# Local attention: the probabilities divided ahead of their transpose, the values held by the array, maximum and exponentials by halves

## The chip, the cores and the metric

One NeuronCore of one Trainium2 chip runs the whole program in one launch. The metric is the device time of that launch in microseconds. PE is TensorE, ACT is ScalarE, DVE is VectorE, POOL is GpSimd, SP is SyncE; PEld is the loading of the array's stationary operand. PSUM is used as four slots R[0] to R[3] of two banks each (128 partitions x 512 float32 a bank).

## The reference, cut to what matters

The program computes four parts one after the other for 32 batches of 128 tokens and 128 channels: a cross-attention, a routed layer of experts, a second cross-attention, and then two layers of the following, which are where the change is. HEADS = 8, DIM_HEAD = 64, WINDOW = 64, all in float32:

```python
h = shift_token(x)                       # second half of the channels from the token before
q, k, v = split(h @ wqkv, 3)             # 128 -> 3 x 512, 8 heads of 64
q, k = l2norm(q) * qs, l2norm(k) * ksc
q, k = rotary_xpos(q, k)
sim = einsum(q * 8, k)                   # per head, keys of this window of 64 and of the one before
sim = where(mask, -max, sim)
attn = softmax(sim)
o = einsum(attn, v)
x = x + o @ wo
# then layernorm of the shifted x, w1, a * gelu(g), w2, and the sum with x
```

The kernel takes each batch of 128 tokens as one 128 x 128 score matrix per head with an additive band mask.

## The kernel before

Each engine runs its own instruction stream, written out by hand, and waits on semaphores. A stage is a software pipeline over the 32 batches: step `i` runs `body(it)`, in which `it.b(lag)` is the batch `i - lag` (or None outside 0 to 31). So one step holds work of several batches, and the order of the blocks in `body` is the order on that engine. Nothing reorders it. The attention of one layer is the four functions `da_tensor`, `da_scalar`, `da_vector` and `da_pool` (and `da_sync` for the DMAs that shift the tokens). `l` is the layer. The layer's second half is `df_*`; `d_into_f` and `f_into_d` join them.

What happens to one batch, with the lag of each step:

- lag 0 to 1: z (the normed x) is written by DVE in the first layer (`d_zn`, L1787) and shifted by two DMAs; PE transposes it (L1650), ACT and DVE split it in a high part (L1719) and a low one (L1779); PE forms q and k in three passes for each half of 512 columns (L461 to L463, called for the columns 0 to 1023) in R[0]; ACT squares them (`d_sq`, L1748).
- lag 2: PE forms v in R[1] (`d_vp`), ACT copies it to SBUF (L1729). DVE multiplies q and k by the rotary tables: A (L1774, 1024 columns) and B in two halves (L1793, 512 columns each), after which it raises `d_rot` to its first count; it sums the squares (`d_ss`, L1810) and bounds them from below (`d_vv`, L1815, a tensor_scalar over 16 columns of SBUF). POOL adds B to A (L1855, waits for the first count of `d_rot`), takes the power -1/2 (L1859, waits for `d_vv`) and scales the keys (L1862).
- lag 4: PE transposes q and k into R[2] (L1630), ACT copies them (L1715), PE adds the band (L1666) and forms the scores of 8 heads in R[2] (L1669, 64 rows each). DVE takes the negated maximum (L1802) and scales it (`d_nm`, L1806). ACT makes the eight exponentials (L743, one per head).
- lag 5: PE transposes the exponentials P into R[3] (L1639), ACT copies them (L1723, `d_pT`). PE forms the product with v, with the transposed P as the stationary operand and v with a 65th column of ones as the moving one, 65 columns (L1686, `d_PV`). DVE takes the reciprocal of the 65th column (L1821) and multiplies the other 64 by it (L1823, `d_on`).
- lag 6: PE transposes the four 128-column pieces of `d_on` (L1680), ACT copies them (L1734, `d_oT`), PE multiplies by wo (L1704), DVE adds the result to Z (L1830).
- lag 7: DVE takes the statistics of the shifted row (L1762, L1038, L1040 `mv`), POOL their root (L1045).

A float32 matmul shows as two instructions of MATMUL, so 8 heads show as x16. A wait such as `e.wait_ge(S("d_exp"), count(b, base=B))` stops the whole engine until the batch `b` has been counted.

Of the kernel before, what the change touches and what calls it, by code (L numbers as in the profile page):

```python
# [112 lines left out]
def program(nc, out, x_in, ctx_in, mask_in, wq0_in, wkv0_in, wo0_in, nrm0_in, wg_in, w1e_in, w3e_in, w2e_in,  # L113
            l1_in, wqkv_in, qks_in, wol_in, lng_in, w1l_in, b1l_in, w2l_in,
            ident_in, band_in, rot_in, keyi_in, head_in):
    with ExitStack() as ctx:
# [184 lines left out]
        d["on"] = at("d_on", [128, 2, 512])  # L301
# [10 lines left out]
        d["v1"] = at("d_v1", [128, 4, HL, 65])  # L312
# [1237 lines left out]
        def c_pool(e):  # L1550
# [3 lines left out]
            e.memset(d["v1"][:, :, :, DL:DL + 1], 1.0).then_inc(S("d_con"), 1)  # L1554
# [62 lines left out]
        def da_tensor(e, l):  # L1617
            t, B = d, NB * l

            def body(it):  # L1620
                if it.static and it.i == 0 and l == 0:
                    e.wait_ge(S("split"), 8)
                    e.wait_ge(S("d_con"), 7)
                b = it.b(4)
                if b is not None:
                    if it.seen(5):
                        e.wait_ge(S("d_exp"), it.upto(5, B))
                    e.wait_ge(S("d_key"), count(b, 3, 3, base=B))
                    for c in range(8):
                        mm = e.transpose(R[2][:, c // 4, 128 * (c % 4):128 * (c % 4) + 128],  # L1630
                                         t["A"][:, it.m(4, 2), 128 * c:128 * c + 128], ident[:])
                    mm.then_inc(S("d_qkTp"), 1)
                b = it.b(5)
                if b is not None:
                    if it.seen(6):
                        e.wait_ge(S("d_div"), nth(it.upto(6, B), 2, 2))
                    e.wait_ge(S("d_exp"), count(b, base=B))
                    for c in range(8):
                        mm = e.transpose(R[3][:, c // 4, 128 * (c % 4):128 * (c % 4) + 128], t["p"][:, it.m(5, 2), c, :], ident[:])  # L1639
                    mm.then_inc(S("d_PT"), 1)  # L1640
# [11 lines left out]
                if b is not None:  # L1652
# [4 lines left out]
                    if it.seen(5):  # L1657
                        e.wait_ge(S("d_max"), nth(it.upto(5, B), 2, 2))
# [3 lines left out]
                if b is not None:  # L1662
# [8 lines left out]
                    mm.then_inc(S("d_S"), 1)  # L1671
                b = it.b(6)
                if b is not None:
# [543 lines left out]
```

## Time and profile before

| | |
|---|---|
| time, median of 3 runs | 1640.44 us (1639.03 to 1648.55) |
| the profiled execution | 1641.26 us; span of its instructions 1639.0 us |
| busy share of the span | PE 90%, PEld 74%, DVE 75%, ACT 68%, POOL 55% |
| granted TensorE clock, mean | 0.968 of full speed |
| chain that ended last | PE 55%, DVE 21%, ACT 7%, the rest under 6% each |

The two attention stages lie between about 900 and 1190 us and between about 1266 and 1565 us of the span. Busy shares are means over stages with different limits, so the rows further down are taken from inside these stages.

### The profile page before, as it was taken

How to read it: one execution, taken by the hardware profiler on the slowest of the kernel's cores; microseconds unless marked ns; L12 is line 12 of the kernel's file. 1: busy time of each engine (PE TensorE's matmuls, PEld its weight loads, DVE VectorE, ACT ScalarE, POOL GpSimd, SP SyncE). 2: the span in 40 equal slices, each digit the busy share in tenths (PEclk: the TensorE clock that was granted, in tenths of full speed). 3: DMA queues.
4: the chain of work that ended last, by engine and by line, in shares of the span. 5: the costliest groups of instructions: out<-in, count | busy, mean ns of one | idle time of the engine just before them, and what ended most of it. 6: DMA issues, size and time to landing. Idle time of an engine off the chain costs nothing.

```text
span 1639.0 us, 37579 instructions
## 1 busy us (share of the span) xinstructions
PE 1477.2 (90%) x11802; PEld 1206.1 (74%) x11803; DVE 1227.3 (75%) x3032; ACT 1112.5 (68%) x2666; POOL 908.3 (55%) x789
## 2 busy tenths in 40 slices
PE   4899999999878998898887899999989799999988
PEld 3677777777757876676665788888877688888866
DVE  6888888888755556878875688888765777878765
ACT  5878888877745556666665687787733687787732
POOL 5667778777740123444431777777600877777600
PEclk9999999999998997979998899999999999999999
DMA  9800000000022320110000000000000000000000
GB/s 382 314 2 7 11 10 11 11 12 16 14 62 68 88 72 21 59 37 21 21 18 10 11 15 15 15 14 15 11 12 4 6 16 14 16 14 15 11 19 38
DMA packets 87336, 62.62 MB, mean 38 GB/s; under 512 B 52037, under 2 KB 72901, under 8 KB 86469
## 3 DMA queue, kind: packets, MB, share of 16 engines
q1 hardware_dynamic: 83141, 53.00, 10.3%
q0 software_dynamic: 4096, 8.40, 1.7%
q8 instruction: 50, 0.82, 0.2%
q14 instruction: 49, 0.40, 0.1%
HBM read 21.30 MB, written 30.41 MB: 32 GB/s over the span
## 4 chain that ended last, share of the span: by engine, by line
PE 55%; DVE 21%; ACT 7%; issue 5%; SPq 5%; POOL 3%; DMA 3%; another core or an unknown queue 1%; DVEq 0%; POOLq 0%; ACTq 0%
PE slot L1686 6%; PE slot L461 5%; SPq L1328 5%; PE slot L463 4%; PE slot L462 4%; PE slot L1669 4%; PE slot L1630 4%; PE slot L1704 3%; PE slot L1639 3%; ACT a_p L743 3%; DMA c_vz<-c_v 3%; DVE a_sum L861 3%; PE slot L1939 2%; POOL a_rq L1106 2%; PE slot L1423 2%
## 5 line engine op out<-in xcount | busy, mean ns | idle before, releaser
L1045 POOL TENSOR_TENSOR rs<-mv,nhalf 128x1 f32 (+1 forms) x160 | 95.9, 599 | 262.0 <-DVE mv L1040 191.5
L1855 POOL TENSOR_TENSOR d_A<-d_A,d_B 128x1024 f32<-128x1024 f32 x64 | 150.9, 2358 | 132.5 <-DVE d_B L1793 132.4
L1859 POOL TENSOR_TENSOR d_r<-d_vv,nhalf 128x16 f32<-128x16 f32 x64 | 186.6, 2916 | 46.9 <-DVE d_vv L1815 46.4
L743 ACT ACTIVATE d_p<-slot,d_nm,d_r 128x128 f32<-128x128 f32 x512 | 186.0, 469 | 27.0 <-DVE d_nm L1806 27.0
L743 ACT ACTIVATE a_p<-slot,a_nm,a_rq 128x77 f32<-128x77 f32 x512 | 163.9, 433 | 57.1 <-DVE a_nm L768 57.1
L743 ACT ACTIVATE c_p<-slot,c_nm 128x77 f32<-128x77 f32 x512 | 117.4, 362 | 20.1 <-DVE c_nm L1478 20.1
L1686 PE MATMUL slot<-d_v,d_pT 128*128 128x65 f32 x1024 | 121.9, 272 | 1.7 <-ACT d_pT L1723 1.7
L1686 PEld LDWEIGHTS slot<-d_v,d_pT 128*128 128x128 f32 x1024 | 119.4, 192 | 2.4 <-ACT d_pT L1723 2.1
L750 POOL TENSOR_TENSOR a_p<-a_p,a_rc 128x616 f32<-128x616 f32 x64 | 80.1, 1252 | 71.2 <-DVE a_rc L863 70.7
L1774 DVE TENSOR_TENSOR d_A<-slot,T 128x1024 f32<-128x1024 f32 x64 | 78.3, 1224 | 47.5 <-PE slot L1630 47.5
L1802 DVE TENSOR_REDUCE slot<-slot 128x8 f32<-128x1024 f32 x64 | 78.9, 1233 | 27.8 <-PE slot L1669 25.1
L1448 ACT ACTIVATE c_pT<-slot 128x768 f32<-128x768 f32 x64 | 52.7, 823 | 67.2 <-PE slot L1370 67.2
L1106 POOL TENSOR_TENSOR a_rq<-a_vvq,nhalf 128x16 f32<-128x16 f32 x32 | 95.0, 2970 | 1.8 <-DVE a_vvq L978 1.8
L626 PE MATMUL slot<-a_kb,a_qT 128*128 128x154 f32 x512 | 81.4, 302 | 11.2 <-DVE a_pT L904 10.8
L1734 ACT ACTIVATE d_oT<-slot 128x512 f32<-128x512 f32 x64 | 38.2, 597 | 78.3 <-PE slot L1680 78.3
L1967 ACT ACTIVATE f_gl<-slot,b1l 128x512 f32<-128x512 f32 (+1 forms) x48 | 32.9, 685 | 77.6 <-PE slot L463 77.6
L1061 POOL DMA_INDIRECT routed<-r_xn,r_ps x64 | 65.0, 1015 | 35.5 <-issue 21.7
L1576 POOL DMA_INDIRECT c_yg<-answers,c_gi x64 | 63.9, 998 | 36.7 <-POOL c_gi L1572 25.5
L626 PEld LDWEIGHTS slot<-a_kb,a_qT 128*128 128x128 f32 x512 | 70.2, 191 | 18.9 <-DVE a_pT L904 17.8
L529 PE MATMUL slot<-ident,a_p 128*77 128x128 f32 x512 | 68.3, 277 | 15.6 <-POOL a_p L750 15.5
L1630 PE MATMUL slot<-ident,d_A 128*128 128x128 f32 x512 | 71.6, 284 | 11.6 <-ACT d_p L743 11.6
L1669 PEld LDWEIGHTS slot<-d_qT 64*128 64x128 f32 x1024 | 62.1, 187 | 27.0 <-issue 27.0
(288 smaller groups left out, 4563.7 us busy)
## 6 DMA issues: line engine op xcount, KB each, us to landing
routed<-zero SPq DMA_DIRECT2D x2, 9216.0 KB, 49.4
b_x<-routed SPq DMA_DIRECT2D x80, 64.0 KB
answers<-b_y SPq DMA_DIRECT2D x40, 128.0 KB
X<-in_x SPq DMA_DIRECT2D x2, 1024.0 KB, 7.2
d_zx<-Z SPq DMA_DIRECT2D x64, 32.0 KB
H<-Z SPq DMA_DIRECT2D x64, 32.0 KB
out<-f_o SPq DMA_DIRECT2D x8, 256.0 KB, 2.0
d_zx<-Z SPq DMA_DIRECT2D x64, 31.8 KB
```

The lines of the kernel that those rows point to most:

```text
L461: e.matmul(o, ws[1], xs[0], start=True, stop=False)
L626: mm = e.matmul(R[slot][:, k // 2, 2 * SK * (k % 2):2 * SK * (k % 2) + 2 * SK], a["qT"][:, c, :], a["kb"][:, it.m(2, 2), c // 2, :], start ...
L743: i = e.activation(t["p"][:, h, :], R[slot][:, k // nbank, nk * (k % nbank):nk * (k % nbank) + nk], ACT.Exp, bias=t["nm"][:, h:h + 1], sca ...
L750: return e.tensor_tensor(p, p, t["rc"][:, h].unsqueeze(2).to_broadcast([128, h.stop - h.start, nk]), ALU.mult)
L1045: return e.tensor_tensor(rs[:, bass.ds(b, 1)], mv[:, bass.ds(b, 1), 1:2].rearrange("p a b -> p (a b)"), nhalf[:, 0:1], ALU.pow)
L1106: e.tensor_tensor(a["rq"][:, it.m(1, 2), :], a["vvq"][:], nhalf[:, 0:16], ALU.pow).then_inc(S("a_rq"), 1)
L1328: e.dma_start(t["vz"][row:row + n, m, c, 32 * j:32 * j + 32], t["v"][key:key + n, m, 32 * j:32 * j + 32])\
L1630: mm = e.transpose(R[2][:, c // 4, 128 * (c % 4):128 * (c % 4) + 128], t["A"][:, it.m(4, 2), 128 * c:128 * c + 128], ident[:])
L1669: mm = e.matmul(R[2][:, h % 2, 128 * (h // 2):128 * (h // 2) + 128], t["qT"][o:o + DL, h // 2, :], t["qT"][o:o + DL, 4 + h // 2, :], start ...
L1686: mm = e.matmul(R[3][:, h // 4, 65 * (h % 4):65 * (h % 4) + 65], t["pT"][:, 4 * (h % 2) + h // 2, :], t["v1"][:, it.m(5, 4), h, :], start= ...
L1855: e.tensor_tensor(t["A"][:, p, :], t["A"][:, p, :], t["B"][:, p, :], ALU.add).then_inc(S("d_key"), 1)
L1859: e.tensor_tensor(t["r"][:, it.m(2, 4), :], t["vv"][:, p, :], nhalf[:, 0:16], ALU.pow).then_inc(S("d_key"), 1)
```

## The change

In each step of the local attention:

- The exponentials write out their sums (`accum_out`, tile `d_sum`), DVE inverts these (SBUF to SBUF), and multiplies the exponentials P themselves, 128 x 1024, in place. This is the first thing on DVE in a step and waits for all exponentials of the step before. `on`, the column of ones and its memset are gone.
- PE transposes P after the scores and not before them, waits for that product, and forms the product with v with v as the stationary operand (128 x 64) and the transposed P as the moving one (128 columns). The two heads of a pair go to partitions 0 to 63 and 64 to 127 of R[3], so the result is already the transpose that wo needs. The four transposes L1680 are gone. ACT copies it (as many columns as L1734). The product with v is now PE's last block of a step, behind the q and k projections.
- Maximum and `d_nm` are made for each bank of R[2], as are the exponentials; ACT copies the transposed P between the two halves, and PE starts each half of the next q and k transposes as soon as the exponentials of that half are done.
- On DVE the second half of B now follows the maxima, the low part of the transposed z follows the first half of B. POOL's code changes only in which count of `d_exp` it waits for.

The diff, without the lines that only rename tiles and counts:

```diff
--- before.py
+++ after.py
@@ -1620,24 +1619,16 @@
...
                 if b is not None:
-                    if it.seen(5):
-                        e.wait_ge(S("d_exp"), it.upto(5, B))
...
                     for c in range(8):
+                        if it.seen(5) and c % 4 == 0:
+                            e.wait_ge(S("d_exp"), nth(it.upto(5, B), c // 4 + 1, 2))
...
                     mm.then_inc(S("d_qkTp"), 1)
-                b = it.b(5)
-                if b is not None:
-                    if it.seen(6):
-                        e.wait_ge(S("d_div"), nth(it.upto(6, B), 2, 2))
-                    e.wait_ge(S("d_exp"), count(b, base=B))
-                    for c in range(8):
-                        mm = e.transpose(R[3][:, c // 4, 128 * (c % 4):128 * (c % 4) + 128], t["p"][:, it.m(5, 2), c, :], ident[:])
-                    mm.then_inc(S("d_PT"), 1)
@@ -1669,23 +1660,24 @@
...
                     mm.then_inc(S("d_S"), 1)
+                b = it.b(5)
+                if b is not None:
+                    if it.seen(6):
+                        e.wait_ge(S("d_oTe"), it.upto(6, B))
+                    e.wait_ge(S("d_div"), count(b, 2, 2, base=B))
+                    for c in range(8):
+                        mm = e.transpose(R[3][:, c // 4, 128 * (c % 4):128 * (c % 4) + 128], t["p"][:, it.m(5, 2), c, :], ident[:])
+                    mm.then_inc(S("d_PT"), 1)
...
                         e.wait_ge(S("d_hl"), it.upto(1, B))
-                    e.wait_ge(S("d_div"), count(b, 2, 2, base=B))
+                    e.wait_ge(S("d_oTe"), count(b, base=B))
                     for c in range(4):
-                        mm = e.transpose(R[1][:, 1, 128 * c:128 * c + 128], t["on"][:, it.m(6, 2), 128 * c:128 * c + 128], ident[:])
-                    mm.then_inc(S("d_OT"), 1)
-                b = it.b(5)
-                if b is not None:
-                    e.wait_ge(S("d_pT"), count(b, base=B))
-                    for h in range(HL):
-                        mm = e.matmul(R[3][:, h // 4, 65 * (h % 4):65 * (h % 4) + 65], t["pT"][:, 4 * (h % 2) + h // 2, :],
-                                      t["v1"][:, it.m(5, 4), h, :], start=True, stop=True)
-                    mm.then_inc(S("d_PV"), 1)
+                        mm = e.matmul(R[1][:, 1, 0:128], t["oT"][:, c, :], wol[:, l, c, :], start=(c == 0), stop=(c == 3))
+                    mm.then_inc(S("d_wo"), 1)
@@ -1697,12 +1689,13 @@
...
                     mm.then_inc(S("d_qkp"), 1)
-                b = it.b(6)
-                if b is not None:
-                    e.wait_ge(S("d_oTe"), count(b, base=B))
-                    for c in range(4):
-                        mm = e.matmul(R[1][:, 1, 0:128], t["oT"][:, c, :], wol[:, l, c, :], start=(c == 0), stop=(c == 3))
-                    mm.then_inc(S("d_wo"), 1)
+                b = it.b(5)
+                if b is not None:
+                    e.wait_ge(S("d_pT"), count(b, base=B))
+                    for h in range(HL):
+                        mm = e.matmul(R[3][DL * (h % 2):DL * (h % 2) + DL, 0, 128 * (h // 2):128 * (h // 2) + 128],
+                                      t["v"][:, it.m(5, 4), h, :], t["pT"][:, 4 * (h % 2) + h // 2, :], start=True, stop=True)
+                    mm.then_inc(S("d_PV"), 1)
@@ -1713,31 +1706,35 @@
...
                     e.activation(t["qT"][:].rearrange("p (a c) t -> p a (c t)", a=2), R[2][:], ACT.Copy).then_inc(S("d_qkT"), 1)
-                b = it.b(1)
-                if b is not None:
-                    e.wait_ge(S("d_zT"), count(b, base=B))
-                    e.activation(t["hT"][0][:, it.m(1, 2), :], z_bank(it), ACT.Copy).then_inc(S("d_hh"), 1)
-                b = it.b(5)
-                if b is not None:
-                    e.wait_ge(S("d_PT"), count(b, base=B))
-                    e.activation(t["pT"][:].rearrange("p (a c) t -> p a (c t)", a=2), R[3][:], ACT.Copy).then_inc(S("d_pT"), 1)
+                b = it.b(6)
+                if b is not None:
+                    e.wait_ge(S("d_PV"), count(b, base=B))
+                    e.activation(t["oT"][:].rearrange("p c t -> p (c t)"), R[3][:, 0, :], ACT.Copy).then_inc(S("d_oTe"), 1)
...
                         e.wait_ge(S("d_PV"), count(b - 4, base=B))
-                    e.activation(t["v1"][:, it.m(2, 4), :, 0:DL], R[1][:, 0, :].rearrange("p (a b) -> p a b", b=DL), ACT.Copy)\
+                    e.activation(t["v"][:, it.m(2, 4), :, :], R[1][:, 0, :].rearrange("p (a b) -> p a b", b=DL), ACT.Copy)\
                         .then_inc(S("d_v"), 1)
-                b = it.b(6)
-                if b is not None:
-                    e.wait_ge(S("d_OT"), count(b, base=B))
-                    e.activation(t["oT"][:].rearrange("p c t -> p (c t)"), R[1][:, 1, :], ACT.Copy).then_inc(S("d_oTe"), 1)
-                b = it.b(4)
-                if b is not None:
-                    e.wait_ge(S("d_max"), count(b, 2, 2, base=B))
...
-                    exponentials(e, {"p": t["p"][:, it.m(4, 2), :, :], "nm": t["nm"]}, 2, 0, 4, 128, S("d_exp"),
-                                 t["r"][:, it.m(4, 4), :], lambda k: 2 * (k % 4) + k // 4)
+                b = it.b(1)
+                if b is not None:
+                    e.wait_ge(S("d_zT"), count(b, base=B))
+                    e.activation(t["hT"][0][:, it.m(1, 2), :], z_bank(it), ACT.Copy).then_inc(S("d_hh"), 1)
+                for half in range(2):
+                    b = it.b(4)
+                    if b is not None:
+                        r = t["r"][:, it.m(4, 4), :]
+                        e.wait_ge(S("d_max"), count(b, 2 * half + 2, 4, base=B))
+                        for j in range(4):
+                            k, h = 4 * half + j, 2 * j + half
+                            ex = e.activation(t["p"][:, it.m(4, 2), k, :], R[2][:, half, 128 * j:128 * j + 128], ACT.Exp,
+                                              bias=t["nm"][:, k:k + 1], scale=r[:, h:h + 1], accum_out=t["sum"][:, k:k + 1])
+                        ex.then_inc(S("d_exp"), 1)
+                    b = it.b(5)
+                    if b is not None and half == 0:
+                        e.wait_ge(S("d_PT"), count(b, base=B))
+                        e.activation(t["pT"][:].rearrange("p (a c) t -> p a (c t)", a=2), R[3][:], ACT.Copy).then_inc(S("d_pT"), 1)
@@ -1764,6 +1761,13 @@
...
                 p = it.m(2, 2)
+                b = it.b(5)
+                if b is not None:
+                    e.wait_ge(S("d_exp"), count(b, 2, 2, base=B))
+                    e.reciprocal(t["rc"][:], t["sum"][:]).then_inc(S("d_div"), 1)
+                    e.wait_ge(S("d_div"), count(b, 1, 2, base=B))
+                    P = t["p"][:, it.m(5, 2), :, :]
+                    e.tensor_tensor(P, P, t["rc"][:].unsqueeze(2).to_broadcast([128, HL, 128]), ALU.mult).then_inc(S("d_div"), 1)
@@ -1772,12 +1776,6 @@
...
                     e.tensor_tensor(A, qk, T1[:, l, :, :].unsqueeze(2).to_broadcast([128, 2, HL, DL]), ALU.mult)
-                b = it.b(1)
-                if b is not None:
-                    e.wait_ge(S("d_hh"), count(b, base=B))
-                    m = it.m(1, 2)
-                    e.tensor_tensor(t["hT"][1][:, m, :], z_bank(it), t["hT"][0][:, m, :].bitcast(F32), ALU.subtract)\
-                        .then_inc(S("d_hl"), 1)
@@ -1789,22 +1787,33 @@
...
                     Bt = t["B"][:, p, :].rearrange("p (a h d) -> p a h d", a=2, d=DL)
-                    for h in range(2):
-                        i = e.tensor_tensor(Bt[:, :, :, 32 * h:32 * h + 32], qk[:, :, :, 32 - 32 * h:64 - 32 * h],
-                                            T2[:, l, :, 32 * h:32 * h + 32].unsqueeze(2).to_broadcast([128, 2, HL, 32]),
-                                            ALU.mult)
-                    i.then_inc(S("d_rot"), 1)
+                    e.tensor_tensor(Bt[:, :, :, 0:32], qk[:, :, :, 32:64],
+                                    T2[:, l, :, 0:32].unsqueeze(2).to_broadcast([128, 2, HL, 32]), ALU.mult)
+                b = it.b(1)
+                if b is not None:
+                    e.wait_ge(S("d_hh"), count(b, base=B))
+                    m = it.m(1, 2)
+                    e.tensor_tensor(t["hT"][1][:, m, :], z_bank(it), t["hT"][0][:, m, :].bitcast(F32), ALU.subtract)\
+                        .then_inc(S("d_hl"), 1)
...
                         e.wait_ge(S("d_v"), it.upto(2, B))
-                    e.tensor_reduce(R[1][:, 0, 0:8], R[2][:].rearrange("p a (j k) -> p a j k", k=128), AX.X, ALU.max, negate=True)\
-                        .then_inc(S("d_max"), 1)
...
-                    e.wait_ge(S("d_max"), count(b, 1, 2, base=B))
-                    e.tensor_tensor(t["nm"][:].rearrange("p (a j) -> p a j", a=2), R[1][:, 0, 0:8].rearrange("p (a j) -> p a j", a=2),
-                                    t["r"][:, it.m(4, 4), 0:8].rearrange("p (j a) -> p a j", a=2), ALU.mult).then_inc(S("d_max"), 1)
+                    for k in range(2):
+                        top = R[1][:, 0, 4 * k:4 * k + 4]
+                        e.tensor_reduce(top, R[2][:, k, :].rearrange("p (j k) -> p j k", k=128), AX.X, ALU.max, negate=True)\
+                            .then_inc(S("d_max"), 1)
+                        e.wait_ge(S("d_max"), count(b, 2 * k + 1, 4, base=B))
+                        e.tensor_tensor(t["nm"][:, 4 * k:4 * k + 4], top,
+                                        t["r"][:, it.m(4, 4), 0:8].rearrange("p (j a) -> p a j", a=2)[:, k, :], ALU.mult)\
+                            .then_inc(S("d_max"), 1)
+                b = it.b(2)
+                if b is not None:
+                    Bt = t["B"][:, p, :].rearrange("p (a h d) -> p a h d", a=2, d=DL)
+                    i = e.tensor_tensor(Bt[:, :, :, 32:64], qk[:, :, :, 0:32],
+                                    T2[:, l, :, 32:64].unsqueeze(2).to_broadcast([128, 2, HL, 32]), ALU.mult)
+                    i.then_inc(S("d_rot"), 1)
@@ -1910,9 +1910,9 @@
...
                         if c == 0:
-                            e.wait_ge(S("d_exp"), count(last))
+                            e.wait_ge(S("d_exp"), count(last, 2, 2))
                         elif c == 1:
-                            e.wait_ge(S("d_div"), count(last, 2, 2))
+                            e.wait_ge(S("d_oTe"), count(last))
```

## Rows read from the trace of the kernel before

**Rows 1.** Busy time by engine in 100 us of each layer's attention.

```profile
core 0: us, PE busy (x) PEld busy (x) DVE busy (x) ACT busy (x) POOL busy (x), PEclk, DMA share, GB/s
1000.00:1100.00 100.00, 100.00 (x820) 86.12 (x818) 83.65 (x170) 79.34 (x157) 76.48 (x47) 1.00 0.07 15
1400.00:1500.00 100.00, 100.00 (x815) 86.67 (x814) 78.82 (x160) 80.13 (x159) 77.64 (x45) 1.00 0.06 14
```

**Rows 2.** Chain that ended last, 1028 to 1038 us: start, length, engine, line.

```profile
1028.41 0.59 PE slot L1680 x4
1028.99 1.73 PE slot L1686 x16
...
1037.26 0.59 PE slot L1680 x4
```

**Rows 3.** Timeline of DVE, one step, first layer: start, length, line.

```profile
1034.16 1.22 DVE L1774 TENSOR_TENSOR d_A<-slot,T 128x1024 f32<-128x1024 f32 x1 [0.65 <-PE slot L1630]
...
1035.65 0.35 DVE L1787 TENSOR_SCALAR Z<-X,mv,rs  x1
1035.91 1.28 DVE L1793 TENSOR_TENSOR d_B<-slot,T 128x512 f32<-128x512 f32 x2
1037.31 1.23 DVE L1802 TENSOR_REDUCE slot<-slot 128x8 f32<-128x1024 f32 x1
1038.58 0.17 DVE L1806 TENSOR_TENSOR d_nm<-slot,d_r 128x8 f32<-128x8 f32 x1
1038.66 1.21 DVE L1810 TENSOR_REDUCE d_ss<-d_sq 128x16 f32<-128x1024 f32 x1
1039.91 0.18 DVE L1815 TENSOR_SCALAR d_vv<-d_ss 128x16 f32<-128x16 f32 x1
1039.99 0.20 DVE L1821 RECIPROCAL d_rc<-slot 128x8 f32<-128x8 f32 x1
1040.23 0.69 DVE L1823 TENSOR_TENSOR d_on<-slot,d_rc 128x512 f32<-128x512 f32 x1
1040.84 0.28 DVE L1762 BATCH_NORM_STATS2 st<-H 128x6 f32 x1
...
1041.58 0.16 DVE L1040 TENSOR_TENSOR mv<-agg,eps 128x2 f32 x1
1042.07 0.29 DVE L1830 TENSOR_TENSOR Z<-Z,slot 128x128 f32 x1 [0.33 <-PE slot L1704]
```

**Rows 4.** Timeline of ACT in the same step.

```profile
1035.24 1.02 ACT L1723 ACTIVATE d_pT<-slot 128x1024 f32<-128x1024 f32 x1
1036.14 0.60 ACT L1729 ACTIVATE d_v<-slot 128x512 f32<-128x512 f32 x1
...
1038.78 2.90 ACT L743 ACTIVATE d_p<-slot,d_nm,d_r 128x128 f32<-128x128 f32 x8 [0.30 <-DVE d_nm L1806]
```

**Rows 5.** Timeline of POOL in the same step.

```profile
1037.28 2.35 POOL L1855 TENSOR_TENSOR d_A<-d_A,d_B 128x1024 f32<-128x1024 f32 x1 [1.24 <-DVE d_B L1793]
1040.24 2.92 POOL L1859 TENSOR_TENSOR d_r<-d_vv,nhalf 128x16 f32<-128x16 f32 x1 [0.61 <-DVE d_vv L1815]
```

**Rows 6.** Timelines of DVE and POOL as the second layer fills, 1275 to 1279 us.

```profile
1275.80 2.34 DVE L1815 TENSOR_SCALAR d_vv<-d_ss 128x16 f32<-128x16 f32 x1
...
1275.75 2.36 POOL L1855 TENSOR_TENSOR d_A<-d_A,d_B 128x1024 f32<-128x1024 f32 x1
```

**Rows 7.** Groups of ACT instructions: count, busy us, mean ns.

```profile
L743 ACT ACTIVATE d_p<-slot,d_nm,d_r 128x128 f32<-128x128 f32 x512 | 186.0, 469 | 27.0 <-DVE d_nm L1806 27.0
...
L1750 ACT ACTIVATE warm<-eps 128x2 f32<-128x2 f32 x2 | 0.4, 204 | 0.0
```

**Rows 8.** Timelines of DVE and POOL in the first cross-attention, about 251 us.

```profile
251.19 0.72 DVE L1040 TENSOR_TENSOR mv<-agg,eps 128x2 f32<-128x2 f32 x1
...
250.68 1.22 POOL L750 TENSOR_TENSOR a_p<-a_p,a_rc 128x616 f32<-128x616 f32 x1 [1.12 <-DVE a_rc L863]
```

**Rows 9.** Timeline of PE there: a product with v held by the array.

```profile
255.77 1.08 PE L549 MATMUL slot<-a_pT,a_vt 77*64 77x256 f32 x8
```

More of the change, by code:

```diff
@@ L300, in program @@
         d["qT"] = at("d_qT", [128, 8, 128])
-        d["on"] = at("d_on", [128, 2, 512])
+        d["sum"] = at("d_sum", [128, 8])
         d["oT"] = at("d_oT", [128, 4, 128])
@@ L311, in program @@
         d["r"] = at("d_r", [128, 4, 16])
-        d["v1"] = at("d_v1", [128, 4, HL, 65])
+        d["v"] = at("d_v", [128, 4, HL, DL])
         squares = room[0]
@@ L1553, in c_pool @@
             e.memset(c_["vz"][:], 0.0).then_inc(S("c_const"), 1)
-            e.memset(d["v1"][:, :, :, DL:DL + 1], 1.0).then_inc(S("d_con"), 1)
             e.memset(d["z"][0:1, :, 64:128], 0.0).then_inc(S("d_con"), 1)
@@ L1622, in body @@
                     e.wait_ge(S("split"), 8)
-                    e.wait_ge(S("d_con"), 7)
+                    e.wait_ge(S("d_con"), 6)
                 b = it.b(4)
                 if b is not None:
-                    if it.seen(5):
-                        e.wait_ge(S("d_exp"), it.upto(5, B))
                     e.wait_ge(S("d_key"), count(b, 3, 3, base=B))
                     for c in range(8):
+                        if it.seen(5) and c % 4 == 0:
+                            e.wait_ge(S("d_exp"), nth(it.upto(5, B), c // 4 + 1, 2))
                         mm = e.transpose(R[2][:, c // 4, 128 * (c % 4):128 * (c % 4) + 128],
@@ L1657, in body @@
                     if it.seen(5):
-                        e.wait_ge(S("d_max"), nth(it.upto(5, B), 2, 2))
+                        e.wait_ge(S("d_max"), nth(it.upto(5, B), 4, 4))
                     passes(e, R[1][:, 0, :], [x[:, it.m(2, 2), :] for x in t["hT"]], [w[:, 1024:1536] for w in wqkv[l]])\
@@ L1815, in body @@
                     e.tensor_scalar(t["vv"][:, p, :], t["ss"][:, p, :], 1e-24, None, ALU.max).then_inc(S("d_rot"), 1)
-                b = it.b(5)
-                if b is not None:
-                    o = R[3][:, :, 0:260].rearrange("p a (j k) -> p a j k", k=65)
-                    rc = t["rc"][:].rearrange("p (a j) -> p a j", a=2)
-                    e.wait_ge(S("d_PV"), count(b, base=B))
-                    e.reciprocal(rc, o[:, :, :, 64]).then_inc(S("d_div"), 1)
-                    e.wait_ge(S("d_div"), count(b, 1, 2, base=B))
-                    e.tensor_tensor(t["on"][:, it.m(5, 2), :].rearrange("p (a j k) -> p a j k", a=2, j=4), o[:, :, :, 0:64],
-                                    rc.unsqueeze(3).to_broadcast([128, 2, 4, 64]), ALU.mult).then_inc(S("d_div"), 1)
                 if not (it.static and it.i >= NB + 5):
@@ L1857, in body @@
                     if past(b - 4):
-                        e.wait_ge(S("d_exp"), count(b - 4, base=B))
+                        e.wait_ge(S("d_exp"), count(b - 4, 2, 2, base=B))
                     e.tensor_tensor(t["r"][:, it.m(2, 4), :], t["vv"][:, p, :], nhalf[:, 0:16], ALU.pow).then_inc(S("d_key"), 1)
@@ L1873, in da_sync @@
             if l == 0:
-                e.wait_ge(S("d_con"), 7)
+                e.wait_ge(S("d_con"), 6)
             def body(it):
```

## Prediction

> **What bounds the kernel now.** I began with the busy times inside the two attention stages, since the page's shares average over all stages. In both layers PE is busy for the whole of 100 us at full clock; DVE, ACT and POOL have 16 to 24% left [rows 1]. The chain of waits says the same: from one group of L1680 to the next it holds PE instructions alone, and 1037.26 - 1028.41 = 8.85 us lie between them [rows 2]. So a step is PE's sum, 8.85 us, in both layers. A step has all its work (batches at lags 2, 4 and 5 at once) for i = 5 to 33, 29 steps in each layer. The change touches only these two stages, so each microsecond of a step is worth 58 us.
>
> The next question is which engine is late once PE has less to do. DVE's timeline gives the length of every instruction, and the distance of two starts is what it costs in a row (its slot). ACT's and POOL's timelines give the same [rows 3 to 5].
>
> **PE.** The transposes of O go: 0.59 us. The product with v took 1.73 us [rows 2]. Its new form streams 16 x 128 columns through a stationary operand of 64 columns, alternating between two halves of the array. The nearest row is L549, 8 x 256 columns in the same alternation, 1.08 us [rows 9]; equally many columns, so I take 1.08. The upper bound is 1.73, if nothing overlaps; nothing suggests less than 1.08. PE's sum becomes 8.85 - 0.59 - 0.65 = 7.61 us, at most 8.26.
>
> **DVE, by its slots** [rows 3]. A step now reads:
> - reciprocal to its user 0.24 (40.23 - 39.99);
> - the product P times 1/sum. No row has 128 x 1024 with both inputs in SBUF; A has the same size with one input in PSUM and takes 1.22, and L1823 with half as many columns 0.69. I take 1.22, as these instructions cost by columns; what could hold it up is a rival below;
> - A and the low part of z, 35.65 - 34.16 = 1.49; Z 0.26 (first layer only); first half of B 0.60. So far 3.81;
> - two maxima of 512 columns. 512 more columns cost 1.22 - 0.69 = 0.53, so half of the 1.23 maximum is 0.70, and 0.04 to `d_nm`; `d_nm` has a slot of 0.08 (38.66 - 38.58). Twice 0.82 = 1.64 in place of 1.35. Now 5.45;
> - second half of B, slot 0.60, length 0.68; sum of squares 1.25; `d_vv` 0.08; statistics 0.74 and `mv` 0.08; Z 0.25.
>
> That is 8.45 us, and 8.19 in the second layer, against 8.86 with 1.2 us of idle now. It would still be under 8.85. But the order has moved.
>
> **What the new order does to `d_vv`.** POOL starts its sum L1855 0.09 after the end of B (37.28 against 37.19) and holds on for 2.35 us. Today maximum, `d_nm` and the squares lie behind B, so `d_vv` starts at 1039.91, 0.28 after POOL has ended [rows 3, 5]. With B's second half behind the maxima only the squares lie between. The trace has that case where the layer fills: `d_vv` started 0.05 after L1855 and took 2.34 instead of 0.18, ending 0.03 after it [rows 6]. So it cannot run beside POOL's sum. In the new step B ends at 5.45 + 0.68 = 6.13, POOL's sum runs from 6.22 to 8.57, `d_vv` reaches the engine at 7.30, ends at 8.60 and lets the next start at 8.50 and not at 7.38: 1.12 us of stall. DVE's step is 8.45 + 1.12 = **9.57 us**, in the second layer **9.31**. Queued behind `d_vv` are the statistics, the sum into Z and the next step's division, and for that one PE's transposes of P.
>
> The Trainium skill, "SBUF — State Buffer", section "Who interferes with whom", says that tensor_scalar can enter modes that take the port pair shared with GpSimd, and then one of the two fully blocks. By that rule `d_vv` waits, and the trace agrees, with its 2.34 us.
>
> **The loop through ACT.** The division waits for all eight exponentials of the batch, and these for the maxima behind it on DVE. The loop is: 3.81 to the first maximum, 0.74, `d_nm` 0.17, 0.03 to ACT (38.78 - 38.75), eight exponentials 2.90, the copy of transposed P between them with a slot of 0.90 (36.14 - 35.24) [rows 4], 0.04 back: 8.59 us, in the second layer 8.33. To this comes eight times x, the price of writing out a sum. No row shows it. Lower bound 0 (it can't make an exponential shorter). If it is an instruction of its own, the smallest that ACT has in this trace took 0.204 [rows 7]. If moreover it cannot overlap, the exponential costs its length of 0.469 in place of its slot (2.90 - 0.47) / 7 = 0.35, so x is up to 0.204 + 0.12 = 0.32. I take 0.20, the nearest row by itself. The loop is then 8.59 + 1.6 = **10.19** and **9.93**, longer than DVE's own sum, so it sets the step, and DVE's stall hides in it.
>
> The skill's "VectorE: DVE Perf Modes", section "Two Vector instructions with no wait between them", counts an operation with an accumulator output as two instructions, the main one and a read; it says so of Vector, and no run here shows ACT.
>
> **Waits that are added and cost nothing.** On PE the q and k projections wait for `d_rot`, now at 6.13, and the product with v is queued behind them; it needs transposed P at 4.74 + 1.45 + 0.8 + 1.0 = 8.0 and ends by 9.1, by 9.8 at the upper price, before the last exponential at 10.15. PE's transposes of P wait for the division (1.46) but stand behind the scores. The copy of O on ACT waits for a product that ended in the step before. POOL's work stays 6.9 us a step.
>
> **The sum.** First layer (10.19 - 8.86) = 1.33, second 1.07: 2.40 x 29 = 70 us. Four further steps (two a layer, where batches run out) have exponentials but no projections; I add 5 us for these, an estimate from 8 x 0.2 less what the halves overlap there. The profiled execution took 1641.26, which is 0.8 over the median: 1641.26 + 75 = **1716 us**, 4.6% more.
>
> **Rivals.**
> - *The sums are free.* x = 0, and DVE's 9.57 and 9.31 decide: (0.71 + 0.45) x 29 = 34 us, 1675. For: ACT may write the sum as it goes. It decides below x = (9.57 - 8.59) / 8 = 0.12. Chance 0.17.
> - *The sums are dear.* x near 0.32: 11.15 and 10.89, (2.29 + 2.03) x 29 + 8 = 133 us, 1774. For: the next exponential overlaps its forerunner today by 0.12, which a read in between could stop. Chance 0.20.
> - *The division waits for POOL's power.* POOL's L1859 runs from 8.65 to 11.57, into the next step, where the product over P has both inputs in SBUF. In the first cross-attention `mv`, also with both in SBUF, was held for 0.72 until POOL's L750 ended [rows 8]. Against: beside L1859 the same `mv` took 0.16 [rows 3, 5], so the power does not hold the port. If it did, the product would wait until 11.57 - T, T = 10.19 + (11.57 - T - 0.24), so T = 10.76, and 10.50 in the second layer: 103 + 5 us, 1749. By the same section of "SBUF — State Buffer" two SBUF inputs contend with any GpSimd instruction that reads SBUF, which would be this case. Chance 0.08.
> - *Faster.* `d_vv` is not held and x is about 0: the loop of 8.59 and 8.33 decides, (0.27 + 0.53) x 29 = 23 us less, 1618. It needs both, x under (8.86 - 8.59) / 8 = 0.03, and B or the squares so late or early that they miss POOL's sum. Against: the 2.34 us row, and that POOL idles before L1855 (1.24 us) and so starts it at once. Chance 0.04.
> - *The columns don't pair.* PE's 8.26 stays under 9.3; the time doesn't move. It is no case of its own.
>
> **How the numbers follow.** The forecast holds 0.47 (x from 0.12 to 0.28, 1675 to 1755), the rivals 0.17, 0.20, 0.08 and 0.04; 0.04 is left for something that I have not seen. The range goes from the free sums, less 7 us for the slots, to the dear ones: 1668 to 1776; out of it lie the faster case, the unseen one and part of the dear one. About 1% is what a measurement of this kernel tells from no change. Faster by over 1%: 0.04. Within 1%: 0.04. Slower: 0.92.
>
> **What would show it.** `d_vv` near 1.3 us in most steps, ending with POOL's L1855; the exponentials' group of eight longer than 2.90 us, or small ACT instructions between them; DVE or ACT, not PE, on the chain in both stages; PE busy near 75 of 100 us there, its product with v at 1.1 us; steps of about 10.2 and 9.9 us. I am wrong if POOL's sum starts so late that `d_vv` goes before it, or if the exponentials keep their 0.35.

## The result, and the profile after

The changed kernel takes 1683.44 us (median of 6 runs, 1676.35 to 1686.91) against 1640.18 us (6 runs, 1638.04 to 1648.55): ratio 1.0254, interval 1.0231 to 1.0277. Its profiled execution took 1685.46 us with a span of 1683.4 us, 44.4 us more than before.

The windows inside the two attention stages, the view of [rows 1], with the kernel after:

```profile
core 0: us, PE busy (x) PEld busy (x) DVE busy (x) ACT busy (x) POOL busy (x), PEclk, DMA share, GB/s
1000.00:1100.00 100.00, 84.53 (x676) 63.58 (x686) 94.72 (x173) 77.15 (x228) 69.99 (x41) 1.00 0.06 13
1400.00:1500.00 100.00, 88.65 (x721) 67.41 (x730) 94.03 (x175) 81.15 (x237) 74.17 (x44) 1.00 0.06 14
```

PE was busy for all 100 us and is now idle for 11 to 15; DVE went from 84 and 79 to 95 and 94. The page says the same for the whole program, in the chain that ended last (before: PE 55%, DVE 21%):

```profile
DVE 38%; PE 23%; issue 15%; ACT 8%; SPq 6%; DMA 3%; POOL 3%; another core or an unknown queue 1%; DVEq 1%; POOLq 0%; ACTq 0%
```

DVE's timeline, one step of the first layer, from `d_vv` to `d_vv`, which answers to [rows 3]:

```profile
1041.05 1.25 DVE L1824 TENSOR_SCALAR d_vv<-d_ss 128x16 f32<-128x16 f32 x1
...
1043.35 0.20 DVE L1767 RECIPROCAL d_rc<-d_sum 128x8 f32<-128x8 f32 x1
1043.58 1.22 DVE L1770 TENSOR_TENSOR d_p<-d_p,d_rc 128x1024 f32<-128x1024 f32 x1
1044.72 1.22 DVE L1778 TENSOR_TENSOR d_A<-slot,T 128x1024 f32<-128x1024 f32 x1
1045.86 0.73 DVE L1785 TENSOR_SCALAR Z<-X,mv,rs  x1
1046.51 0.68 DVE L1790 TENSOR_TENSOR d_B<-slot,T 128x512 f32<-128x512 f32 x1
1047.11 0.27 DVE L1796 TENSOR_TENSOR d_hTl<-slot,d_hTh 128x128 fp32r<-128x128 f32 x1
1047.31 0.68 DVE L1805 TENSOR_REDUCE slot<-slot 128x4 f32<-128x512 f32 x1
1048.03 0.16 DVE L1808 TENSOR_TENSOR d_nm<-slot,d_r 128x4 f32<-128x4 f32 x1
...
1048.91 0.68 DVE L1814 TENSOR_TENSOR d_B<-slot,T 128x512 f32<-128x512 f32 x1
1049.51 1.21 DVE L1819 TENSOR_REDUCE d_ss<-d_sq 128x16 f32<-128x1024 f32 x1
1050.75 1.34 DVE L1824 TENSOR_SCALAR d_vv<-d_ss 128x16 f32<-128x16 f32 x1
1052.01 0.28 DVE L1759 BATCH_NORM_STATS2 st<-H 128x6 f32 x1
```

POOL's timeline in the same step, which answers to [rows 5]:

```profile
1042.47 2.91 POOL L1859 TENSOR_TENSOR d_r<-d_vv,nhalf 128x16 f32<-128x16 f32 x1 [0.20 <-DVE d_vv L1824]
1045.46 1.04 POOL L1862 TENSOR_TENSOR d_A<-d_A,d_r 128x512 f32<-128x512 f32 x1
...
1049.67 2.40 POOL L1855 TENSOR_TENSOR d_A<-d_A,d_B 128x1024 f32<-128x1024 f32 x1 [2.65 <-DVE d_B L1814]
1052.28 2.92 POOL L1859 TENSOR_TENSOR d_r<-d_vv,nhalf 128x16 f32<-128x16 f32 x1 [0.21 <-DVE d_vv L1824]
```

Read the two side by side. `d_vv` starts on DVE at 1050.75 and ends at 1052.09, with POOL's L1855 (1052.07): 1.34 us instead of 0.18. I call this a hold: an instruction that has started, but ends only with the other engine's. There is a second one, which I had not foreseen: Z starts at 1045.86, 0.40 after POOL's L1862 began, and ends at 1046.59, with L1862 at 1046.50: 0.73 instead of 0.35. And one that did not come: the division L1770, both inputs in SBUF, takes 1.22 while POOL's power L1859 runs, and L1859 keeps its 2.9. DVE waits in this step only for its own results (0.31 us in the statistics), so its queue is the step. The distances from `d_vv` to `d_vv` are 9.70 to 9.91 us in the first layer, mean 9.80, and in the second 9.04 to 9.14 with every fourth 9.57 to 9.60, mean 9.22; before it was 8.86 in both.

ACT's timeline of the same step, which answers to [rows 4]:

```profile
1045.60 0.35 ACT L1723 ACTIVATE d_hTh<-slot 128x128 fp32r<-128x128 f32 x1
1048.22 0.46 ACT L1731 ACTIVATE d_p<-slot,d_nm,d_r 128x128 f32<-128x128 f32 x1 [2.28 <-DVE d_nm L1808]
1048.58 0.19 ACT L1731 ACTIVATION_READ_ACCUMULATOR d_p<-slot,d_nm,d_r 128x1 f32 x1
1048.67 0.45 ACT L1731 ACTIVATE d_p<-slot,d_nm,d_r 128x128 f32<-128x128 f32 x1
```

and the exponentials' two groups of ACT on the page, which answer to [rows 7]:

```profile
L1731 ACT ACTIVATE d_p<-slot,d_nm,d_r 128x128 f32<-128x128 f32 x512 | 228.3, 466 | 128.9 <-DVE d_nm L1808 128.9
...
L1731 ACT ACTIVATION_READ_ACCUMULATOR d_p<-slot,d_nm,d_r 128x1 f32 x512 | 109.0, 213 | 0.0
```

Writing out a sum is an instruction of its own, 213 ns long. But it starts before the exponential has ended, and the next exponential before it has: the distance from one exponential to the next is 0.44 to 0.45 (1048.67 - 1048.22), against 0.35 before. So a sum costs x = 0.09 us (x is the prediction's name for this price). ACT idles for 2.28 us a step and waits for DVE.

### The profile page after: what moved, and what is told of

Same layout as the page of the kernel before. It is cut to its first block, busy times and chain, and to the rows that moved or that the text cites. A ratio compares the mean times of both kernels' runs of the same rounds, so it can differ in the third digit from the quotient of the medians.

```text
span 1683.4 us, 37884 instructions
## 1 busy us (share of the span) xinstructions
PE 1434.0 (85%) x11484; PEld 1117.3 (66%) x11547; DVE 1338.2 (79%) x3160; ACT 1142.6 (68%) x3178; POOL 910.5 (54%) x788
## 4 chain that ended last, share of the span: by engine, by line
DVE 38%; PE 23%; issue 15%; ACT 8%; SPq 6%; DMA 3%; POOL 3%; another core or an unknown queue 1%; DVEq 1%; POOLq 0%; ACTq 0%
SPq L1328 5%; DVE slot L1805 5%; DVE d_A L1778 4%; DVE d_ss L1819 4%; DMA c_vz<-c_v 3%; PE slot L461 3%; ACT a_p L743 3%; DVE a_sum L861 3%; ACT d_p L1731 2%; PE slot L1939 2%; POOL a_rq L1106 2%; PE slot L1423 2%; DVE a_ssq L971 2%; PE slot L463 2%; PE slot L462 2%
## 5 line engine op out<-in xcount | busy, mean ns | idle before, releaser
L1731 ACT ACTIVATE d_p<-slot,d_nm,d_r 128x128 f32<-128x128 f32 x512 | 228.3, 466 | 128.9 <-DVE d_nm L1808 128.9
L1855 POOL TENSOR_TENSOR d_A<-d_A,d_B 128x1024 f32<-128x1024 f32 x64 | 153.0, 2390 | 205.5 <-DVE d_B L1814 205.5
L1859 POOL TENSOR_TENSOR d_r<-d_vv,nhalf 128x16 f32<-128x16 f32 x64 | 186.5, 2914 | 11.7 <-DVE d_vv L1824 9.9
L1731 ACT ACTIVATION_READ_ACCUMULATOR d_p<-slot,d_nm,d_r 128x1 f32 x512 | 109.0, 213 | 0.0
L1805 DVE TENSOR_REDUCE slot<-slot 128x4 f32<-128x512 f32 x128 | 88.2, 689 | 7.9 <-PE slot L1660 7.7
L1824 DVE TENSOR_SCALAR d_vv<-d_ss 128x16 f32<-128x16 f32 x64 | 83.6, 1306 | 4.7
L1745 ACT ACTIVATE d_sq<-slot 128x1024 f32<-128x1024 f32 x64 | 67.5, 1054 | 22.8 <-PE slot L463 19.4
L1696 PE MATMUL slot<-d_pT,d_v 128*64 128x128 f32 x1024 | 71.7, 283 | 12.0 <-ACT d_pT L1737 12.0
```

Source lines behind the costliest of these rows:

```text
L1731: ex = e.activation(t["p"][:, it.m(4, 2), k, :], R[2][:, half, 128 * j:128 * j + 128], ACT.Exp, bias=t["nm"][:, k:k + 1], scale=r[:, h:h + ...
L1805: e.tensor_reduce(top, R[2][:, k, :].rearrange("p (j k) -> p j k", k=128), AX.X, ALU.max, negate=True)\
L1824: e.tensor_scalar(t["vv"][:, p, :], t["ss"][:, p, :], 1e-24, None, ALU.max).then_inc(S("d_rot"), 1)
L1855: e.tensor_tensor(t["A"][:, p, :], t["A"][:, p, :], t["B"][:, p, :], ALU.add).then_inc(S("d_key"), 1)
L1859: e.tensor_tensor(t["r"][:, it.m(2, 4), :], t["vv"][:, p, :], nhalf[:, 0:16], ALU.pow).then_inc(S("d_key"), 1)
```

## The experiments

A loop, here, is a chain of instructions on several engines in which each waits for the one before and the last for itself one step earlier; a step can't be shorter than its longest loop. Two theories. **D**: DVE's own queue decides, lengthened by `d_vv` and Z, which cannot run beside POOL's L1855 and L1862. **L**: the loop through ACT decides (exponentials with their sums, division, A, maximum), as my prediction had it. Each group ran on one chip beside the kernel before: 1634.93 us (7 runs) for the labels e1 to e4, 1610.05 (15 runs) for e4b, e5, e6 and e8. So ratios are compared, not times.

**The holds taken away.** In the changed kernel `d_vv` becomes a tensor_reduce: the maximum over pairs, each of a sum and 1e-24.

```diff
-e.tensor_reduce(t["ss"][:, p, :], t["sq"]..., AX.X, ALU.add)
-e.tensor_scalar(t["vv"][:, p, :], t["ss"][:, p, :], 1e-24, None, ALU.max)
+e.tensor_reduce(t["ss"][:, p, :, 0], t["sq"]..., AX.X, ALU.add)      # ss[..., 1] holds 1e-24
+e.tensor_reduce(t["vv"][:, p, :], t["ss"][:, p, :, :], AX.X, ALU.max)
```

> The changed kernel with one instruction in another form: d_vv, the bound of the 16 sums from below, is made by a tensor_reduce (maximum of each sum and a constant beside it) and not by a tensor_scalar; same result, same place in the order. Theory H (VectorE's own sum sets the step, 9.80 us in the first layer and 9.12 in the second, 1.2 us of it the hold of d_vv behind POOL's sum): d_vv falls from 1.31 us to about 0.17, the statistics' mv is now caught by the end of POOL's sum for some 0.3, and the step falls until the loops through ScalarE decide: about 9.45 and 9.0 us, so (0.35 + 0.12) x 29 = 14 us less, 1669. Rival L (a loop through the exponentials already sets the step): d_vv is shorter and the time stays within 3 us of 1683. Rival P (any small instruction beside POOL's sum is held): d_vv keeps 1.3 us, 1683.

Measured: 1669.41 us, ratio 1.0197 (1.0157 to 1.0236). Steps 9.55 and 9.11 us. DVE and POOL in the timeline of the first layer:

```profile
1043.72 1.21 DVE L1820 TENSOR_REDUCE d_ss<-d_sq 128x16 f32<-128x1024 f32 x1
1044.97 0.19 DVE L1825 TENSOR_REDUCE d_vv<-d_ss 128x16 f32<-128x32 f32 x1
1045.27 0.30 DVE L1760 BATCH_NORM_STATS2 st<-H 128x6 f32 x1
...
1046.22 0.28 DVE L1831 TENSOR_TENSOR Z<-Z,slot 128x128 f32 x1
1047.02 0.20 DVE L1768 RECIPROCAL d_rc<-d_sum 128x8 f32<-128x8 f32 x1 [0.52 <-ACT d_p L1732]
...
1049.53 0.82 DVE L1786 TENSOR_SCALAR Z<-X,mv,rs  x1
```

```profile
1043.89 2.40 POOL L1856 TENSOR_TENSOR d_A<-d_A,d_B 128x1024 f32<-128x1024 f32 x1 [2.65 <-DVE d_B L1815]
```

In the middle of POOL's sum the same maximum as a reduce takes 0.19. But 1.1 us of stall gave back 0.25 and 0.11 us a step: a new wait of 0.52 for the exponentials stands before the division. In the first layer both theories hold, one behind the other: D at 9.80, L at 9.55 (with Z held for 0.82 in it). In the second layer DVE waits once more behind the division, 0.20 for the scores, so that the division doesn't decide there; what does is found below. The Trainium skill, "SBUF — State Buffer", section "Who interferes with whom", says that on trn2 a tensor_reduce never contends with GpSimd; the 0.19 agrees.

Next, Z is moved as well, behind the second maximum, where POOL idles:

```diff
 # DVE: division, A
-Z (L1786)
 # B's first half, low part of z, maxima
+Z (L1810)
 # B's second half, squares, d_vv
```

> The kernel of e1_vv_reduce, and besides the first layer's Z (tensor_scalar, 0.73 to 0.77 us where it took 0.35 before) is moved from behind A to behind the second maximum, where POOL is idle. Theory H with a second hold: Z is held by POOL's L1862, and moved it takes 0.35 again; in the first layer 0.40 of hold and 0.26 of slot leave the loop from division to exponentials, so its step falls to about 9.0 us, 0.45 x 29 = 13 us under e1: 1656. Second layer as in e1. Rival (Z is longer for another reason, its place or its operands): it stays at 0.7 us and the time at that of e1.

Measured: 1665.63 us, ratio 1.0182 (1.0142 to 1.0221); steps 9.39 and 9.10. A miss: I had expected 9.0 in the first layer. Z is back at 0.35, but B's second half now starts 0.53 after the start of the second `d_nm` and not 0.07, and PE's q and k projections wait for it, with the product with v and the next transposes behind them. PE and ACT in the first layer:

```profile
1049.14 0.50 PE L461 MATMUL slot<-wqkv0h,d_hTl 128*128 128x512 f32 x1 [0.94 <-DVE d_B L1815]
```

```profile
1043.50 1.03 ACT L1709 ACTIVATE d_qT<-slot 128x1024 f32<-128x1024 f32 x1 [0.18 <-PE slot L1630]
```

This gave 0.16 us a step. With Z elsewhere there were 0.44 to be had, as the next run shows.

Z goes first instead, before the division, so that B isn't delayed:

```diff
+Z (L1771)
 # DVE: division (L1776, L1779), A, B's first half, ...
-Z (L1786)
```

> The kernel of e1_vv_reduce with the first layer's Z as the first instruction of VectorE's step, ahead of the division, where VectorE waits for the exponentials and POOL is in its power. Theory: in the first layer neither Z's hold nor its slot lies on a loop any more, and B, with the projections that wait for it, is no later than in e1; so the first layer's step is the second's, 9.1 to 9.2 us (9.55 in e1, 9.38 in e2): about 10 us under e1, ratio to before 1.013. Rival (PE's projections behind B set e2's 9.38 in any order): as e2, ratio 1.018.

Measured: 1631.70 us, ratio 1.0126 (1.0101 to 1.0151). Steps 9.11 in both layers: Z takes 0.34 and DVE is busy for 89.39 and 85.89 of 100 us. The two holds were worth 1.3% of the time, half of the loss. By steps: (0.69 + 0.11) x 29 = 23 us, and 1.28% of 1640 is 21.

What sets its 9.11? DVE now waits inside the step, and ACT runs through from the exponentials to the copy of q and k. Its DVE, then its ACT:

```profile
1045.83 0.70 DVE L1806 TENSOR_REDUCE slot<-slot 128x4 f32<-128x512 f32 x1 [0.21 <-PE slot L1661]
```

```profile
1042.05 1.06 ACT L1746 ACTIVATE d_sq<-slot 128x1024 f32<-128x1024 f32 x1
1042.96 1.07 ACT L1709 ACTIVATE d_qT<-slot 128x1024 f32<-128x1024 f32 x1
...
1046.76 0.46 ACT L1732 ACTIVATE d_p<-slot,d_nm,d_r 128x128 f32<-128x128 f32 x1 [1.59 <-DVE d_nm L1809]
```

It is a loop over R[2]: squares 0.91, copy of q and k and the scores up to the maximum 2.87 (1045.83 - 1042.96), maximum and `d_nm` 0.93, then eight exponentials with their sums at 0.44 and the copy of transposed P at 0.91, together 4.4: 9.1. I had not listed this one; it shares the exponentials with L, but goes back through PE's scores and not through the division. The second run without sums, below, shortens its exponentials and so tests it.

**The sums taken away.** The exponentials lose `accum_out`, and the reciprocal reads a constant tile, so P is multiplied by a constant and the softmax isn't normalized. From the changed kernel:

```diff
-..., scale=r[:, h:h + 1], accum_out=t["sum"][:, k:k + 1])
+..., scale=r[:, h:h + 1])
-e.reciprocal(t["rc"][:], t["sum"][:])
+e.reciprocal(t["rc"][:], nhalf[:, 0:8])
```

> The changed kernel without the sums of the exponentials: no accumulator output, and the reciprocal is taken of a constant tile, so that the division has the wrong factor but the same size and place. 512 instructions ACTIVATION_READ_ACCUMULATOR go, and the exponential's slot falls from 0.44 to 0.35. Theory H: the sums are hidden behind VectorE, steps stay at 9.8 and 9.12, time 1683 within 3 us. Rival L, that of the prediction (8 x 0.09 to 8 x 0.2 a step on the loop that sets it): at least 0.7 x 58 = 41 us less, 1642 or under.

Measured: 1675.38 us, ratio 1.0242 (1.0204 to 1.0280). Steps 9.79 and 9.22: the same as with the sums. In the changed kernel the sums are hidden, L doesn't decide there, and D does.

The same edit on top of the version with Z first:

> The kernel of e6_z_first without the accumulator outputs; the reciprocal is of a constant tile, so the division's factor is wrong and its size and place are kept. With VectorE's holds gone the theory is that a loop through ScalarE decides (exponentials, squares, copy of q and k, scores, maximum, exponentials). Then the eight sums, which cost nothing in e3, cost 8 x 0.09 = 0.72 us a step: steps of about 8.4 us, 42 us under e6, near 1620, ratio 0.99. Rival (VectorE's own sum of about 8.1 to 8.4 plus waits, or PE, sets the step at about 9): within 5 us of e6.

Measured: 1616.50 us, ratio 1.0031 (1.0015 to 1.0048). Steps 8.92 and 8.92. Here the sums do cost, 0.19 us a step, but not the 8 x 0.09 = 0.72 by which ACT got shorter: another wait took their place, seen in the timelines of ACT and PE.

```profile
1048.81 1.07 ACT L1746 ACTIVATE d_sq<-slot 128x1024 f32<-128x1024 f32 x1
1050.32 1.02 ACT L1709 ACTIVATE d_qT<-slot 128x1024 f32<-128x1024 f32 x1 [0.44 <-PE slot L1630]
```

```profile
1046.58 0.50 PE L461 MATMUL slot<-wqkv0h,d_hTl 128*128 128x512 f32 x1 [0.48 <-DVE d_B L1815]
...
1048.17 1.09 PE L1697 MATMUL slot<-d_pT,d_v 128*64 128x128 f32 x16
1049.19 1.09 PE L1630 MATMUL slot<-ident,d_A 128*128 128x128 f32 x8
```

PE's q and k projections wait for B's second half, the product with v follows, then the next transposes of q and k, for which ACT waits 0.44. That loop goes over maximum, B, projections, product with v, transposes, copy and scores back to the maximum. Its pieces, from one maximum to the next: 2.35 to the first projection (1046.58 - 1044.23, where the maximum starts), 1.59 to the product with v, 1.02 to the transposes, 1.13 to the copy and 2.83 to the next maximum, together 8.92. I made no run that shortens it. But the run with Z behind the maximum lengthened its first piece by 0.46, and 8.92 + 0.46 = 9.38 against its measured 9.39.

**B's place alone.** In the kernel before, only B's second half is moved behind `d_nm`:

```diff
 # DVE: A, low part of z, Z, B's first half
-B's second half (L1793)
 # maximum (L1802), d_nm (L1806)
+B's second half
 # squares, d_vv
```

> The kernel before with one move alone: the second half of B behind maximum and d_nm, as in the change; nothing else of it. POOL's sum then starts at about 39.4 in the step of the rows and d_vv comes at 40.5, so theory H says that it is held for about 1.2 us, 64 times. VectorE's step becomes 7.6 + 1.2 = 8.8, still under PE's 8.86: time 1640 within 4 us. Rival (the hold costs wherever it is): 1.2 x 58 = 70 us more, 1710. A small loss of up to 10 us would say that PE's projections, which wait for B, come just too late.

Measured: 1664.83 us, ratio 1.0156 (1.0109 to 1.0203), steps 9.32 in both layers. I had expected no change; that was a miss. The second layer's timeline, DVE, then POOL (its sum L1855 is L1859 in this file), then PE:

```profile
1443.73 1.23 DVE L1819 TENSOR_SCALAR d_vv<-d_ss 128x16 f32<-128x16 f32 x1
1444.88 0.20 DVE L1825 RECIPROCAL d_rc<-slot 128x8 f32<-128x8 f32 x1
...
1446.64 0.29 DVE L1834 TENSOR_TENSOR Z<-Z,slot 128x128 f32 x1
```

```profile
1442.55 2.38 POOL L1859 TENSOR_TENSOR d_A<-d_A,d_B 128x1024 f32<-128x1024 f32 x1 [2.37 <-DVE d_B L1809]
```

```profile
1445.86 1.08 PE L1639 MATMUL slot<-ident,d_p 128*128 128x128 f32 x8
1447.06 0.33 PE L1650 MATMUL slot<-ident,d_zx 128*128 128x128 f32 x1
```

DVE still has idle time (it waits 0.58 us for the scores before the maximum of this step and 0.86 in the next) and could have absorbed more. But `d_vv` lies before the sum into Z, and PE's L1650 waits for that sum (`d_add`): it ends at 1446.93, L1650 starts at 1447.06 and not right behind L1639, whose eight take 0.88 up to the next instruction in the kernel before. Of the 1.1 us of hold 0.46 a step reached PE, which was full. (In the first layer Z is held as well, for 1.09 us, and DVE doesn't wait for PE.)

The hold taken out of that kernel, `d_vv` as a reduce as above:

> The kernel of e4_b_late (before, with B's second half behind the maximum), with d_vv as a tensor_reduce. e4 cost 30 us, which my expectation for it missed: its trace says that the hold delays VectorE's last instruction, the sum into Z, for which PE's transpose of the next z waits. If the hold is the cause, it goes here and PE decides again: 8.86 us a step, ratio to before 1.000 within 0.003. If it was B's place itself (PE's projections wait for it), the ratio stays at 1.016.

Measured: 1611.52 us (10 runs), ratio 1.0010 (1.0001 to 1.0020), steps 8.86, and in the first layer Z takes 0.34 again. So the 1.6% was the hold; the new place of B itself costs about 0.1%, and at most 0.2%.

**B early in the changed kernel.** Both halves before the maxima, so that POOL's sum ends before `d_vv`:

```diff
 # DVE: division, A, Z, B's first half
+B's second half (L1792)
 # low part of z, maxima
-B's second half (L1814)
 # squares, d_vv
```

> The changed kernel with one move: both halves of B ahead of the maxima, as in the kernel before. POOL's sum then starts about 2.2 us earlier in the step and d_vv must be free again (0.18 us). Theory W (the place of B is a wash): the 1.15 us of hold go, but 0.60 us of B enter the loop from division over maxima and exponentials back to the division, which in the second layer of the changed kernel was 0.35 short of deciding (8.77 of 9.12): 8.77 + 0.60 = 9.37 there, and 9.6 in the first layer. Time as the changed kernel's, ratio to before 1.025 within 0.005. Rival H (the hold is the price of the change): 1.15 x 58 = 66 us less, ratio 0.985.

Measured: 1656.77 us, ratio 1.0277 (1.0254 to 1.0300), the same as the change itself within the intervals. Steps 9.66 and 9.40. The holds are gone and a longer loop is in their place; DVE, then POOL (the product L1862 is L1859 in this file):

```profile
1043.18 0.34 DVE L1785 TENSOR_SCALAR Z<-X,mv,rs  x1
...
1047.77 0.17 DVE L1821 TENSOR_SCALAR d_vv<-d_ss 128x16 f32<-128x16 f32 x1
...
1050.32 0.20 DVE L1767 RECIPROCAL d_rc<-d_sum 128x8 f32<-128x8 f32 x1 [1.02 <-ACT d_p L1731]
```

```profile
1041.47 1.56 POOL L1859 TENSOR_TENSOR d_A<-d_A,d_r 128x512 f32<-128x512 f32 x1
```

B's second half (0.60) now stands between division and maximum, so the exponentials start later and the next division waits 1.02 us for them. This is L, and the only version in which it sets both layers' step. So in the changed kernel B late or early costs the same: late it brings the holds, early it lengthens L.

## Why the prediction was right, and where it wasn't

The forecast was 1716 us with a range from 1668 to 1776; measured 1683.44. Direction and range held, the size was 33 us too high.

- **PE.** Right in what matters: the product with v takes 1.09 us (I took 1.08), and PE is no longer full. The sign "PE busy near 75 of 100 us" did not come: 84.53 and 88.65, which is 8.28 and 8.17 us a step where I had summed 7.61. Some blocks are longer than before (the transposes of q and k take 1.23 in the step from 1041, 1.09 before); why stays open, and PE doesn't set the step.
- **DVE's sum, 8.45 us in the first layer.** 0.23 too high: 9.80 less 1.18 for `d_vv` (1052.01 - 1050.75, less 0.08) and 0.40 for Z is 8.22. I had taken the length of the product over P, 1.22, where it costs 1.14 in a row (1044.72 - 1043.58), and 1.49 for A and the low part of z, a distance that held idle time; they cost 1.14 and 0.20. In the second layer the step is 9.10 without the odd fourth one, with a hold of 1.08, where I had 9.31.
- **The hold of `d_vv`, 1.12 us.** Right in place, cause and size; the first run above shows it by itself.
- **The loop through ACT, 10.19 and 9.93 us: the step that failed.** The term that was mis-sized is x: 0.20 taken, 0.09 measured. I took the length of a small ACT instruction (0.204; the real one has 0.213) for its cost in a row. With 0.09 the loop is 8.59 + 0.72 = 9.31 and 9.05, below DVE's own 9.57 and 9.31, so by the prediction's own threshold (0.12) the rival "the sums are free" applied, with 1675. The run without sums shows it: 1.0242 against 1.0254. Without a hold L is shorter still: with B early it is 9.66 and 9.40, and 0.60 of that is B's second half, so it is 9.06 and 8.80 in the order of the changed kernel (the 0.23 above is a part of this loop too). A further loop through the exponentials, the one over R[2], was missing from my list.
- **Luck.** 1683 lies inside the span that I gave my own case (1675 to 1755), but the loop on which that case rests did not decide. The path was that of a rival to which I had given 0.17, and the time came out above the rival's only by what follows.
- **What that rival lacked** is 8 to 10 us. Steps: (9.80 - 8.86) x 29 + (9.22 - 8.86) x 29 = 27.3 + 10.4 = 37.7 of the span's 44.4. The hold of Z is in it (0.40 x 29 = 12 us), largely made up by my DVE sums, which were too high (0.23 x 29 = 7 us in the first layer, 0.09 x 29 = 3 us in the second). The other 7 lie where the layers fill and drain. 4 of them arose behind the end of the first layer's attention: PE's work of the layer's second half starts 26 us later than before and ends 30 us later. There the granted clock fell: 0.83 in the window 1180 to 1230 us, with 0.54 from 1196 to 1206, so that it was at its lower level, 1.2 GHz, for most of those 10 us. In the two stretches of 10 us before that, PE was busy for 8.03 and 7.92 us. In the kernel before the clock was 1.00 in this part of the program (1150 to 1200 us, PE busy for 44.48 of 50). That the clock took the 4 us was not tested.
- **The division waits for POOL's power.** Fell: 1.22 us beside L1859.
- **Sums dear.** Fell.
- **Faster.** Fell: even with both holds and the sums gone, the steps are 8.92, not under 8.86. The prediction had it decided by L at 8.59. But PE's projections wait for B's second half, a wait that I had put down as costing nothing. Beside a step of 10.2 us that would be so, but its loop alone is 8.92, over the 8.86 of before.
- **Open:** why every fourth step of the second layer is 0.45 longer. Four steps are one pass of the loop in the code. The long step is there without the sums, and gone with the reduced `d_vv`, where DVE no longer sets the step. DVE is idle before the reciprocal there, 0.24 us that the trace puts to issue, and I made no run on it.

So where did PE's 1.24 us a step go? Three bounds lie close above what it would need, each found when the one before was gone: DVE's queue with its two holds (9.80 and 9.22), the loop over R[2] with the sums (9.11), and the one through PE's projections and B (8.92). The first two are shown by runs that take them away, the third by its sum and by the run that lengthened it. Before, PE alone decided at 8.86, and no version here is faster than that.

## What to carry to other kernels

When an edit relieves a full engine, work out each loop that crosses the engines, and not only each engine's sum: the gain ends at the next one, here 0.06 us above the old bound. A small instruction placed beside another engine's long one can cost that one's whole length; where it is queued, and who waits for what stands behind it, decides who pays, and changing its form (here a reduce) may be enough. The length of an instruction that is new to a kernel is not yet its price: what counts is what it adds to the distance of its neighbours, here 0.09 us for one of 0.213. Before there is a row for that, keep both as cases.

## What the runs showed of the hardware

- A tensor_scalar of 16 columns was held until L1855 had ended (1.31 us on average), one of 128 columns until L1862 had (0.73 to 0.77 instead of 0.35, and up to 1.10 with B late in the kernel before). A tensor_reduce of 32 columns took 0.19 in the middle of L1855.
- A tensor_tensor can be held too: with the reduced `d_vv`, `mv` of 2 columns took 0.27 instead of 0.16 and ended with POOL's sum (1046.30 and 1046.29).
- It goes the other way too. With B early, POOL's scaling of the keys (1.04 us elsewhere) took 1.56 to 1.67, having started at 1041.47 under DVE's division L1770 (1040.90 to 1042.13), which has both inputs in SBUF. The Trainium skill, "SBUF — State Buffer", section "Who interferes with whom", says that whoever issues first gets the pair of ports that DVE and GpSimd share, and the other blocks, and that two SBUF inputs contend with a GpSimd instruction that reads SBUF. The first agrees. The second holds for `mv` and for the scaling of the keys, but not for POOL's power, which reads SBUF too: division and power ran side by side at their usual 1.22 and 2.9 us.
- An accumulator output on ACT is an instruction of 213 ns of which 0.09 us shows, at 128 columns.
